# Masks fetched as one-hot rows beside the Gram rows, in an orthogonal matching pursuit kernel

## The reference, cut to what matters

```
x = x + conv3x3(group_norm(x))            # ternary weights, two convolutions folded into one
z = group_norm(x)
X = 4x4 patches of z (all 32 channels)    # 512 values per patch, 256 patches per image
D = dictionary / norm of its columns      # 512 x 256 atoms
coeffs = batch_omp(X, D)                  # 5 greedy steps
x = x + patches(D @ coeffs)
```

## Time and profile before

| | |
|---|---|
| median of 3 runs | 542.66 us (541.69 to 544.27) |
| the profiled execution | 542.04 us, span 540.2 us |
| mean granted TensorE clock | 0.905 of full |
| busy: PE, DVE, ACT, POOL | 75%, 85%, 57%, 28% |
| chain that ended last | PE 47%, DVE 35%, ACT 6%, issue 6%, SP queue 4% |
| indirect DMAs on POOL | 128 |

### The profile page before, as it was taken

One profiled execution on the slowest core, in us unless ns is written; L12 is line 12 of the kernel. 1 busy time (PEld: TensorE's weight loads), 2 busy tenths in 40 slices (PEclk: granted clock), 3 DMA queues, 4 the chain that ended last, 5 costly groups with the idle time before them and its releaser, 6 DMA issues.

```text
span 540.2 us, 7421 instructions
## 1 busy us (share of the span) xinstructions
PE 403.2 (75%) x1666; PEld 291.6 (54%) x1666; DVE 457.6 (85%) x2323; ACT 309.0 (57%) x682; POOL 149.2 (28%) x162
## 2 busy tenths in 40 slices
PE   0089884999756669999874889998939466788674
PEld 0033772455655656458773755567828355676453
DVE  4574657899799989999999799999998999899990
ACT  2635537876556379778666498676803343465133
POOL 3000035343200064534200655423004644230010
PEclk9999996999779689999996979999979976899598
DMA  5989912799400035999400473413101844134165
GB/s 97 173 101 170 158 39 59 124 161 161 81 0 2 0 88 118 188 178 179 108 1 1 102 171 83 113 40 90 29 1 49 189 113 110 48 78 85 33 116 117
DMA packets 110202, 50.71 MB, mean 94 GB/s; under 512 B 103632, under 2 KB 104144, under 8 KB 110160
## 3 DMA queue, kind: packets, MB, share of 16 engines
q1 hardware_dynamic: 102000, 26.13, 30.9%
q0 software_dynamic: 8160, 24.13, 19.6%
HBM read 34.24 MB, written 8.65 MB: 79 GB/s over the span
## 4 chain that ended last, share of the span: by engine, by line
PE 47%; DVE 35%; ACT 6%; issue 6%; SPq 4%; DMA 1%; DVEq 0%; ACTq 0%
PE h L374 30%; PE conv_ps L374 13%; DVE junk L978 9%; DVE coef L1099 5%; DVE top L908 4%; DVE top_i L921 3%; PE back_ps L374 3%; SPq L241 3%; DVE top_i L923 2%; ACT score L623 2%; ACT diag L632 2%; DVE mask L1005 1%; DVE coef L1095 1%; ACT xb L589 1%; DMA d_sb<-in_L_conv_dictionary 1%
## 5 line engine op out<-in xcount | busy, mean ns | idle before, releaser
L346 POOL DMA_INDIRECT rows<-gram,idx_u x128 | 130.9, 1022 | 334.2 <-DVEq L965 304.7
L374 PE MATMUL h<-rows,diag 128*128 128x256 f32 x640 | 159.7, 408 | 42.3 <-ACT diag L632 41.6
L374 PEld LDWEIGHTS h<-rows,diag 128*128 128x128 f32 x640 | 128.8, 205 | 74.0 <-issue 53.3
L632 ACT ACTIVATE diag<-ident,dx 128x128 f32<-128x128 f32 x320 | 96.8, 388 | 42.1 <-DVEq L1080 39.3
L978 DVE SCALAR_TENSOR_TENSOR junk<-mask,rows 128x256 bf16<-128x256 bf16 x320 | 118.9, 416 | 0.0
L623 ACT ACTIVATE score<-h 128x512 f32<-128x512 f32 x80 | 47.3, 597 | 98.1 <-PE h L374 97.3
L908 DVE MAX8 top<-score 128x8 f32<-128x256 f32 x160 | 65.0, 419 | 22.9 <-ACT score L623 20.9
L374 PE MATMUL back_ps<-coef_t,d_t 128*128 128x256 f32 x224 | 58.3, 419 | 14.5 <-ACT coef_t L638 14.5
L374 PE MATMUL h<-d_sb,z 128*128 128x256 f32 x256 | 66.1, 421 | 3.4 <-DVEq L899 2.5
L374 PEld LDWEIGHTS h<-d_sb,z 128*128 128x128 f32 x256 | 62.8, 329 | 6.7 <-issue 3.2
L374 PE MATMUL conv_ps<-xa,w_taps 128*64 128x512 f32 x128 | 62.7, 613 | 0.1
(11 more groups left out here) (144 smaller groups left out, 491.0 us busy)
## 6 DMA issues: line engine op xcount, KB each, us to landing
xa<-in_x SPq DMA_DIRECT2D x64, 128.0 KB, 4.5
out<-x SPq DMA_DIRECT2D x64, 128.0 KB, 2.9
x<-y POOLq DMA_DIRECT2D x14, 512.0 KB, 4.7
xb<-in_x SPq DMA_DIRECT2D x48, 128.0 KB
rows<-gram,idx_u POOLq DMA_INDIRECT x128, 2.9
xb<-in_x SPq DMA_DIRECT2D x16, 120.0 KB
d_sb<-in_L_conv_dictionary SPq DMA_DIRECT2D x4, 128.0 KB, 4.0
gram<-coef_t SPq DMA_DIRECT2D x1, 256.0 KB, 2.6
```

The costliest lines, as they stand in the source:

```text
L346: pool.indirect_dma_start(out=rows[s][:, k, t, :], out_offset=None, in_=gram_dram[:, :], in_offset=bass.IndirectOffsetOnAxis(ap=idx_u[s][: ...
L374: return nc.tensor.matmul(dst, lhs, rhs, start=start, stop=stop, skip_group_check=skip)
L632: last = nc.scalar.activation(diag[s][:, t, j, :], ident[:, :], ACT.Copy, scale=dx[s][:, k, t, j:j + 1])
```

## The change

Six edits go together.

1. A 256x256 identity in bf16 (`one_hot`) is made by POOL in the setup, stored to HBM by SP ahead of the Gram matrix, and `gather_masks(s, k)` fetches its rows (512 bytes each) by the same indices as the Gram rows: the masks of steps 0, 1 and 2. Those of half 0 are issued right behind `gather(r, 0, k)`, those of half 1, step k-1, behind `gather(r, 1, k)`.
2. `extract` makes no mask in steps 1 and 2. The picks of these steps compare the iota with the index themselves.
3. The second index reduction into `idx_0` in step 0 is gone.
4. ScalarE writes the first term of each coefficient row (`begin_coef`: mask of step 0 times x). `spread` has 8 operations an image, and waits for ScalarE and for the masks.
5. A semaphore `x_last_ready` tells ScalarE that the coefficients of a half are there.
6. `mask` holds 5 steps; for its room KEPT goes from 11 to 10.

The diff, cut to its core:

```diff
-    KEPT = 11
+    KEPT = 10
+    GATHERED = 3
...
+        one_hot_dram = nc.dram_tensor("one_hot", [ATOMS, ATOMS], BF16, kind="Internal").ap()
...
-        mask = [sb(f"mask{s}", [P, STEPS - 1, TILES, ATOMS], BF16) for s in range(2)]
+        mask = [sb(f"mask{s}", [P, STEPS, TILES, ATOMS], BF16) for s in range(2)]
...
+        one_hot = coef[:, 0, 0, :].bitcast(BF16).rearrange("p (k a) -> p k a", k=CHUNKS)
...
+            sp.wait_ge(const_done, 1)
+            sp.dma_start(one_hot_dram.rearrange("(k p) a -> p k a", p=P), one_hot).then_inc(one_hot_stored, 16)
             sp.wait_ge(gram_sb_done, 1)
...
+            step(nc.gpsimd.memset(one_hot, 0.0))
...
+            for k in range(CHUNKS):
+                put_ones(one_hot[:, k, :], k * P)
...
+            def gather_masks(s, k):
+
+                for t in range(TILES):
+                    pool.indirect_dma_start(out=mask[s][:, k, t, :], out_offset=None, in_=one_hot_dram[:, :],
+                                            in_offset=bass.IndirectOffsetOnAxis(ap=idx_u[s][:, k, t:t + 1], axis=0)
+                                            ).then_inc(masks_in[s], 16)
...
                         gather(r, s, k)
+                        if s == 0 and k < GATHERED:
+                            gather_masks(0, k)
+                        if s == 1 and k > 0:
+                            gather_masks(1, k - 1)
                         if r > 1 and (k, s) == (0, 0):
                             add_back(IMG_R * (r - 1) - 1)
...
+            def begin_coef(r, m):
+                s = m // 2
+                act.wait_ge(x_last_ready[s], r + 1)
+                act.wait_ge(masks_in[s], 16 * TILES * (GATHERED * r + 1))
+                if r > 0:
+                    act.wait_ge(coef_t_ps, IMG_R * (r - 1) + m + 1)
+                for t in range(2):
+                    tile = 2 * (m % 2) + t
+                    last = nc.scalar.activation(coef[:, m, t, :], mask[s][:, 0, tile, :], ACT.Copy, scale=x_last[s][:, tile, 0:1])
+                last.then_inc(coef_begun, 1)
...
                 if behind:
                     copy_coef(b, 0)
+                    begin_coef(b, 2)
+                    begin_coef(b, 3)
                 scores(r, 1, 0)
...
                     norm_y(f, 2)
                     norm_y(f, 3)
+                begin_coef(r, 0)
+                begin_coef(r, 1)
+                if front:
                     scores(f, 0, 0)
...
             for m in range(IMG_R):
+                if m == 2:
+                    begin_coef(ROUNDS - 1, 2)
+                    begin_coef(ROUNDS - 1, 3)
                 copy_coef(ROUNDS - 1, m, final_ps)
...
-                    step(v.tensor_reduce(idx_0[s][:, r % 2, :], top_i[s][:, :, 0:2], AX.X, ALU.min))
...
-                c = step(v.scalar_tensor_tensor(out=place, in0=mask_of(r, s, k, t), scalar=1.0,
-                                                in1=source, op0=ALU.mult, op1=ALU.mult, accum_out=dst))
+                if k < GATHERED:
+                    c = step(v.scalar_tensor_tensor(out=place, in0=iota_short[:, :], scalar=idx_u[s][:, k, t:t + 1],
+                                                    in1=source, op0=ALU.is_equal, op1=ALU.mult, accum_out=dst))
...
-                for t in range(TILES):
+                for t in range(TILES if k >= GATHERED else 0):
...
-                if r > 0:
-                    dve.wait_ge(coef_t_ps, IMG_R * (r - 1) + m + 1)
-                for j in range(STEPS):
+                dve.wait_ge(coef_begun, IMG_R * r + m + 1)
+                dve.wait_ge(masks_in[s], 16 * TILES * GATHERED * (r + 1))
+                for j in range(1, STEPS):
```

More of the change, by code:

```diff
@@ L105, in build_program @@
         idx_u = [sb(f"idx_u{s}", [P, STEPS, TILES], U32) for s in range(2)]
-        idx_0 = [sb(f"idx_0{s}", [P, 2, TILES]) for s in range(2)]
         is_best = [sb(f"is_best{s}", [P, TILES, 8]) for s in range(2)]
@@ L196, in build_program @@
         coef_ready = sem("coef_ready")
+        coef_begun = sem("coef_begun")
+        one_hot_stored = sem("one_hot_stored")
+        masks_in = [sem(f"masks_in{s}") for s in range(2)]
+        x_last_ready = [sem(f"x_last_ready{s}") for s in range(2)]
         coef_t_ps = sem("coef_t_ps")
@@ L348, in gather @@
                                             ).then_inc(rows_in[s][t], 16)
+            def gather_masks(s, k):
[3 more added lines that the diff above has]
+                                            ).then_inc(masks_in[s], 16)
             pool.wait_ge(gram_stored, 16)
+            pool.wait_ge(one_hot_stored, 16)
             def add_back(n):
@@ L967, in mask_of @@
             def mask_of(r, s, k, tile):
-                return mask[s][:, k - 1, tile, :]
+                return mask[s][:, k, tile, :]
             junk_n = [0]
@@ L977, in pick @@
                 place = junk[:, junk_n[0] % JUNK, :]
-                c = step(v.scalar_tensor_tensor(out=place, in0=mask_of(r, s, k, t), scalar=1.0,
-                                                in1=source, op0=ALU.mult, op1=ALU.mult, accum_out=dst))
+                if k < GATHERED:
+                    c = step(v.scalar_tensor_tensor(out=place, in0=iota_short[:, :], scalar=idx_u[s][:, k, t:t + 1],
+                                                    in1=source, op0=ALU.is_equal, op1=ALU.mult, accum_out=dst))
+                else:
+                    c = step(v.scalar_tensor_tensor(out=place, in0=mask_of(r, s, k, t), scalar=1.0,
+                                                    in1=source, op0=ALU.mult, op1=ALU.mult, accum_out=dst))
                 junk_c[junk_n[0] % JUNK] = c
@@ L1012, in extract @@
                             dve.wait_ge(rows_in[s][t], 16 * ((STEPS - 1) * r + j + 1))
-                        if j == 0:
+                        if j == 0 and marked:
                             after(marked[t])
@@ L1081, in solve @@
                 else:
-                    step(v.tensor_reduce(x_last[s][:, :, :], dx[s][:, :, :, :].rearrange("p k t j -> p t j k"), AX.X, ALU.add))
+                    c = step(v.tensor_reduce(x_last[s][:, :, :], dx[s][:, :, :, :].rearrange("p k t j -> p t j k"), AX.X, ALU.add))
+                    yield
+                    after(c)
+                    dve.sem_inc(x_last_ready[s], 1)
             def spread(r, m):
                 s = m // 2
-                if r > 0:
-                    dve.wait_ge(coef_t_ps, IMG_R * (r - 1) + m + 1)
-                for j in range(STEPS):
+                dve.wait_ge(coef_begun, IMG_R * r + m + 1)
+                dve.wait_ge(masks_in[s], 16 * TILES * GATHERED * (r + 1))
+                for j in range(1, STEPS):
                     added = []
@@ L1092, in spread @@
                         tile = 2 * (m % 2) + t
[L1093 to L1097, removed]
+                        if j > 1:
                             after(before[t])
-                            added.append(step(v.scalar_tensor_tensor(out=coef[:, m, t, :], in0=mask_of(r, s, j, tile), scalar=x,
-                                                                     in1=coef[:, m, t, :], op0=ALU.mult, op1=ALU.add)))
+                        added.append(step(v.scalar_tensor_tensor(out=coef[:, m, t, :], in0=mask_of(r, s, j, tile),
+                                                                 scalar=x_last[s][:, tile, j:j + 1],
+                                                                 in1=coef[:, m, t, :], op0=ALU.mult, op1=ALU.add)))
                         yield
```

## The result

The changed kernel takes 563.32 us (median of 4 runs, 562.04 to 565.93), the kernel before 542.86 beside it: 1.0391 times as long, 95% interval 1.0356 to 1.0426. The forecast was 553.1 with a range of 547 to 560. So the sign was right and the size was not: 20.5 us where 10.5 were forecast.

The account below looks back on a forecast made before the run. TensorE was taken to pace steps 0 to 3 of rounds 0 to 2, the vector engine the round ends, both alternating in round 3. 542.04 - 2.4 + 0.1 + 11.0 + 1.8, plus 0.6 for the median, gave 553.1 us (range 547 to 560).

Parts of the forecast that it names:

- (d) KEPT 10: Body 1: `out_conv(2,3)` on ScalarE waits for image 1's store, issued behind input loads; +11.0 us.
- Rival B: The stall is no stall: image 1's stores land in time or other work covers the wait; 542.2 us, chance 0.07.
- (b): Ends of rounds 0 to 2: shorter `spread` ahead of image 0's coefficient transposes gains 0.8 us each, -2.4 us.
- rival A: The vector engine paces all rounds, so all 18.0 us of saved vector work reach the end; 535.7 us, chance 0.04.
- (a): Vector engine: masks and coefficient rows leave it, picks cost 0.05 us more each (4.8); net 18.0 us less work.
- (e) the queue of POOL: 96 more gathers on POOL make Gram rows late in round 3 only; +1.8 us, between -3.2 and +8.
- The first row lands 2.9 later: Body 1, half 1 of step 2: POOL reaches the Gram rows at 238.4, the first lands at 241.3.
- Hidden by 1.4 us, and rounds 0 and 2 look alike: Those body 1 rows land 1.4 us before TensorE wants them at 242.74; rounds 0 and 2 likewise.
- A sign that the prediction had named as showing it wrong: Updates in body 2 waiting for gathered rows would show the forecast wrong; no size given.
- Rival C: POOL is worse: fours of 6.2 us or Gram rows landing later; 562 us, more likely 557.7, chance 0.14.
- (c) ScalarE's rows: ScalarE's added coefficient operations cost 0 in the bodies; in the last reconstruction they lose what `spread` saves, +0.1 us.
- The Trainium skill's rule on gathers beside two-port vector work: GpSimd cannot write descriptors during two-port VectorE operations; if each four gained 0.3 us, the +1.8 would be about 0.

Follow-up runs that it names:

- best: masks_late_tail with image 1's store one image earlier, ahead of the loads of m = 2: 540.76 us (ratio 0.9961).
- masks_late_tail: store_early with all mask gathers behind each round's steps, and ScalarE's last rows of images 2 and 3 ahead of image 1's last `out_back`: 542.42 us.
- store_early: The changed kernel with image 1's store ahead of the last image's input loads: 634.94 us, with engines waiting for instructions.
- kept10_store: The kernel before with KEPT 10 and image 1's store ahead of the loads of m = 2: 542.26 us (ratio 0.9988).
- kept10: The kernel before with only KEPT changed from 11 to 10: 557.55 us (ratio 1.0186).
- tail_swap: store_early with ScalarE copying image 1's coefficients before beginning the rows of images 2 and 3 in the last reconstruction: 550.1 us (ratio 1.0158).
- after_again: The changed kernel, unaltered, run once more in the second comparison: 562.01 us (ratio 1.0343).
- store_early_again: The same kernel as store_early, run once more in the second comparison: 551.35 us (ratio 1.0163).
- add_back_first_again: store_early with each step's mask gathers behind its `add_back` instead of ahead of it: 551.5 us (ratio 1.0143).
- half1_late: store_early with half 1's mask gathers alone moved behind the steps of each round: 551.64 us (ratio 1.0140).

## Why the prediction was wrong

- **(d) KEPT 10**, +11.0: right. 10.7 by the store's place, 11.6 by the constant alone, 11.16 on ScalarE; best against masks_late_tail adds some 1.8 that store_early had left. `reconstruct(1,2)` took 6.25 us for its 16 matmuls at a granted clock of 0.50, as the prediction thought possible. Rival B had nothing for it.
- **(b)**, -2.4: the right mechanism, and somewhat too much. The gap before the transposes in bodies 1 to 3 is 26.9 us after 28.4, so 0.5 each and not 0.8, 1.5 in all. best has all costs moved away and is 1.5 us below kept10_store, which has the same store and none of the vector work's savings. The 15.5 us that VectorE lost reach the end no further; rival A is out.
- **(a)**, picks at +0.05 each: they take 479 ns against 415, so 0.064 each, above the upper bound of 0.058. For 96 picks that is 6.1 us and not 4.8, on an engine that does not set the pace there.
- **(e) the queue of POOL**: this is the step that failed, at the words "The first row lands 2.9 later" and "Hidden by 1.4 us, and rounds 0 and 2 look alike". What the queue does was right: 998 ns a mask gather, 0.30 between, and POOL came to round 3's rows of half 0, step 2, at 469.46, which is 451.1 in the frame of before, just as forecast. The landing was not: 2.9 us is the median over the span, while gathers issued in body 1 beside the input loads landed after 7.1 to 7.7. And only half 1's rows of step 2 were looked at, not half 0's, which had 0.6 us of slack. With the prediction's own queue: POOL idle at 205.6, four fours (two of rows, two of masks) and an `add_back` are 22.2 us, so 227.8; plus 7.7 is 235.5, against a use at 231.57: 3.9 us late. Measured 3.7, and then 2.9 more because the update ran at the lower clock. These 6.7 us and kept10's 11.3 would give 18.0 for body 1, against the 16.5 measured; the remaining 1.5 is not accounted for. In round 3 the rows of half 0, step 2, were used 4.4 us after their issue and not 2.9, so the update began 3.3 us later than before (52.0 after 48.7 from the round's start) and not 1.8; what that cost is not shown, as said above. By the runs all gathers in the steps cost 7.4 us (tail_swap at +6.8, masks_late_tail at -0.6) where 1.8 was forecast.
- A sign that the prediction had named as showing it wrong, an update in body 2 that waits for rows, came: 0.52 us in the changed kernel, 1.11 in after_again.
- Rival C had this direction ("Gram rows landing later") and a chance of 0.14, and its upper price, 562, is within 1.3 us of the result. That is luck: it put 6.2 more on round 3, 3 on rounds 0 and 2 and nothing on body 1.
- **(c) ScalarE's rows**: no cost in the bodies, as forecast; in the last reconstruction 2.3 us in the trace, 1.5 by tail_swap, instead of 0.1. The forecast let `out_back` of image 1 move 0.64 earlier with `spread(3,0)`. Counted from the first transposes it ends where it did (14.65 after 14.64), and the gap before these transposes shrank by 0.10 only (4.39 after 4.49). So the vector engine begins its eight operations 0.7 late (15.41 after 14.69), and the lower clock behind it adds 1.7 (5.41 after 3.72), for which the sum had no term.
- The Trainium skill's rule on gathers beside two-port vector work (page "SBUF — State Buffer", section "SBUF: two separate sides") would have made the gathers quicker. With half the masks gone from VectorE a gather of rows takes 984 ns after 1022, 38 ns less, so 0.15 a four and not the 0.3 weighed there; in kept10_store, with all masks, it takes 1032. The runs bear out little of it.

Taken together, each run against the kernel before of its comparison: best stands at -2.3; the rest of the stall (masks_late_tail) adds 1.8, the gathers in the steps (tail_swap) 7.4, ScalarE's place (store_early_again) 1.5, and the store's place (after_again) 10.7, which makes the 19.0 measured there. The forecast had -2.4, 11.0 for the stall's 12.4, 1.8 for 7.4 and 0.1 for 1.5. The sum closes because it is a chain of differences; the store's 10.7 is within one comparison, the other steps cross comparisons, and those of 1.5 and 1.8 have overlapping intervals. Open stays how the 7.4 us divide among the rounds, and among late rows and the lower clock behind them: add_back_first_again and half1_late took off a half or more of the waits for rows and won nothing, so the waits on TensorE are not a sum that can be handed back one by one.

## What to carry to other kernels

Read a transfer's landing in the stretch where it happens, not over the span: here the same gather took 2.9 us in the median and 7.1 to 7.7 beside the loads, and that alone turned "hidden by 1.4 us" into a late update. Look also at the tightest consumer in the queue and not at one of them. When commands are added to a queue that also feeds a tight consumer, put them where nobody waits behind them (here at the round's end), and see who needs them first there, and what is issued behind them: here an `add_back` that ScalarE and the output stores waited for. A ring of buffers shortened by one is free only if each reuse has its transfer issued ahead of work that depends on the reuse.

## What the runs showed of the hardware that was not expected

- In the kernel before, gathers of 128 rows landed in a median of 5.8 us beside input loads alone (100:124), 7.1 beside loads and an accumulating transfer of 512 KB (215:240), and 2.8 beside such transfers without loads (300:352). In the changed kernel rows were used 7.6 us after their issue in body 1, though POOL had issued the four in 0.94 to 1.06 us each.
- After 3.06 us of idleness of TensorE the granted clock was 0.50 in 237.51:240, and 24 matmuls took 8.37 us instead of 5.45: the wait cost nearly twice its length. In the last reconstruction a wait of 1.62 us instead of 0.92, then four transposes and 0.69 us of idleness, was followed by 0.63 (546.62:549), and 16 matmuls took 5.41 instead of 3.72: here 0.7 us more of waiting cost 2.4. After 1.16 us (285.04) 23 matmuls took 5.20, as at the full clock.
- Round 3 takes 101.5 us at a granted clock of 0.85 (kernel before) and 104.75 at 0.81 (kept10_store), with no gathers added in either.
- The same kernel took 634.94 us in one comparison and 551.35 in another, with ScalarE and VectorE waiting up to 11.8 us for an instruction, while the kernel before beside it moved by 3 us. What brings these waits on was not found.
